# Mixture of experts over 64 experts: how the routing weights reach the tokens, and how far the down projection lags

## The reference, cut to what matters

```
xf = x.reshape(T, D)                                   # T = 4096, D = 128
shared = silu(xf @ Ws_up) @ Ws_down                    # F = 64
aff = xf @ centroids.T                                 # E = 64
_, idx = top_k(aff + expert_biases, 8)
w = sigmoid(take_along_axis(aff, idx)); w = w / (w.sum(-1) + 1e-8)
cw = zeros((T, E)).at[arange(T)[:, None], idx].add(w)
h = silu(einsum('td,edf->etf', xf, W_up))
y = einsum('etf,efd->etd', h, W_down)
out = x + shared + einsum('etd,te->td', y, cw)
```

## Time and profile before

| | us |
|---|---|
| median of 3 runs | 1128.03 (1126.86 to 1128.64) |
| the profiled execution | 1126.31 |
| its span, first to last instruction | 1124.5 |
| last stage | from 662.6 to the end |

### The profile page before, as it was taken

How to read it: one execution, slowest core, us unless ns; L and a number is a source line. 1 busy time by engine, 2 the same in 40 slices (tenths; PEclk the granted TensorE clock), 3 DMA queues, 4 the chain that set the end, 5 groups by cost and what they waited for, 6 DMA issues and landing times.

```text
span 1124.5 us, 20697 instructions
## 1 busy us (share of the span) xinstructions
PE 981.0 (87%) x6164; PEld 779.5 (69%) x6164; DVE 846.1 (75%) x1938; ACT 723.8 (64%) x1416; POOL 439.8 (39%) x503
## 2 busy tenths in 40 slices
PE   5665089999658999999999989999999999999998
PEld 3444079999536777776776667777777677777776
DVE  4865577777568888888887667878787768787865
ACT  4543045555347778778777667777777667777775
POOL 0266750000156556555553303333333333333343
PEclk9555589999869999999999989999999999999999
DMA  9011122222211101101010013241414140505050
GB/s 251 18 45 46 65 58 65 64 66 66 68 28 24 34 20 29 29 23 36 20 30 11 1 43 86 50 87 44 92 36 101 35 103 12 124 12 125 12 124 10
DMA packets 59749, 61.68 MB, mean 55 GB/s; under 512 B 15973, under 2 KB 54022, under 8 KB 57606
## 3 DMA queue, kind: packets, MB, share of 16 engines
q1 hardware_dynamic: 54976, 52.02, 19.4%
q0 software_dynamic: 4096, 8.40, 2.4%
q10 hardware_dynamic: 582, 0.09, 0.0%
HBM read 45.73 MB, written 14.75 MB: 54 GB/s over the span
## 4 chain that ended last, share of the span: by engine, by line
PE 74%; DVE 12%; ACT 5%; issue 5%; POOL 1%; DMA 1%; SPq 1%; DVEq 0%; POOLq 0%; ACTq 0%
PE ps L2070 5%; PE ps L2048 5%; PE ps L2050 4%; PE ps L2049 4%; PE ps L2072 4%; PE ps L2071 4%; PE ps L1848 4%; PE ps L1791 3%; PE ps L1911 3%; PE ps L2057 3%; PE ps L1866 3%; PE ps L1894 3%; PE ps L1872 2%; PE ps L1770 2%; PE ps L1769 2%
## 5 line engine op out<-in xcount | busy, mean ns | idle before, releaser
L741 POOL TENSOR_TENSOR hl<-h,hh 128x512 fp32r<-128x512 f32 x128 | 165.7, 1294 | 309.0 <-ACT hh L1017 309.0
L1017 ACT ACTIVATE hh<-h 128x512 fp32r<-128x512 f32 (+1 forms) x264 | 165.0, 625 | 17.4 <-DVE h L1634 16.1
L1534 DVE TENSOR_REDUCE nm<-ps 128x4 f32<-128x512 f32 (+1 forms) x128 | 116.3, 951 | 35.6 <-PE ps L1894 33.7
L1634 DVE TENSOR_TENSOR h<-sg,ps 128x512 f32<-128x512 f32 x160 | 108.2, 676 | 39.5 <-ACT sg L1005 37.9
L1005 ACT ACTIVATE sg<-ps 128x512 f32<-128x512 f32 x160 | 95.7, 598 | 54.4 <-PE ps L2050 54.2
L645 POOL DMA_INDIRECT yg<-ys,gps x64 | 63.0, 984 | 168.6 <-issue 158.1
L2070 PE MATMUL ps<-hh,wh 128*128 128x512 f32 x256 | 103.6, 405 | 18.0 <-DVE hl L1641 17.0
L2048 PE MATMUL ps<-xh,wh 128*128 128x512 f32 x256 | 105.8, 413 | 0.0
L1634 DVE TENSOR_TENSOR h<-ps,cwB 128x512 f32<-128x512 f32 x96 | 65.8, 685 | 50.2 <-ACT ps L1005 45.7
L1641 DVE TENSOR_TENSOR hl<-h,hh 128x512 fp32r<-128x512 f32 (+1 forms) x136 | 93.0, 684 | 13.6 <-ACT hh L1017 13.6
L2050 PE MATMUL ps<-xh,wl 128*128 128x512 f32 x256 | 102.7, 401 | 0.0
(11 more groups left out here) (320 smaller groups left out, 2741.1 us busy)
## 6 DMA issues: line engine op xcount, KB each, us to landing
cwB<-cwd SPq DMA_DIRECT2D x16, 1536.0 KB, 10.8
xb<-xs SPq DMA_DIRECT2D x72, 64.0 KB, 1.8
ys<-yb SPq DMA_DIRECT2D x72, 64.0 KB, 1.6
cwd<-cwS SPq DMA_DIRECT2D x32, 96.0 KB
x_res<-in_L_attn_x_dram SPq DMA_DIRECT2D x4, 512.0 KB, 9.1
wst<-in_L_ffn_W_up_dram SPq DMA_DIRECT2D x32, 64.0 KB, 2.2
wst<-in_L_ffn_W_down_dram SPq DMA_DIRECT2D x32, 64.0 KB, 1.9
out_dram<-y SPq DMA_DIRECT2D x8, 256.0 KB, 4.9
```

The source lines that it names most:

```text
L741: pool.tensor_tensor(hl4[:, u % 3, :], h4[:, u % 3, :], hh4[:, u % 3, :].bitcast(F32), op=ALU.subtract).then_inc(u_hlp, 1)
L1017: act.activation(hh4[r, u % 3, :], h4[r, u % 3, :], ACT.Copy).then_inc(u_hh, 1)
L1534: ins = dve.tensor_reduce(nm[:, u, 4 * g:4 * g + 4], o, axis=AX.X, op=ALU.max, negate=True)
L1634: dve.tensor_tensor(h4[:, u % 3, :], first, second, op=ALU.mult).then_inc(u_h, 1)
```

## The change

The diff has these parts in the last stage:

- NS goes from 20 to 8, NB from 12 to 24: units 1 to 8 are spread units, 9 to 32 are broadcast units.
- cwd has CWR = 4 copies instead of 8 and holds four pieces of 6 pairs (NPC); cwB has three buffers of 6 units (NBUF). SP writes with four DMAs of 48 rows each, then issues three loads (`spread_rows`) and the fourth (`rows_again`) once h of unit 14 has been made, since it goes to the buffer of the first. `e_h` waits for a load at units 9, 15, 21 and 27.
- Broadcast units rotate over five banks (0 to 4) for their up projections; spread units keep three and two.
- h and its two parts have five buffers (one of them for unit 0), and LAG is 4.
- The copy of the weights on DVE orders them by piece. cwS has 64 rows.

Beside it, the load of wuT (attention's output weights) moves behind the second stage and to other SBUF, and GpSimd's three semaphores for its own links become one.

```diff
-        NS = 20
+        NS = 8
         NB = NP2 - NS
         EP, EB = 2 * NS, 2 * NB
-        HB = 32
-        CWR = 8
-        assert EB <= HB and HB + 2 * EP <= P and NB % 2 == 0
-        cwd = nc.dram_tensor("cwd", [2, 2, 2, CWR, NB // 2 * TT], F32).ap()
+        HB = 64
+        CWR = 4
+        NPC, NBUF = 4, 3
+        G = NB // NPC
+        assert EB <= HB and HB + 2 * EP <= P and NB % NPC == 0
+        cwd = nc.dram_tensor("cwd", [2, NPC, 2, CWR, G * TT], F32).ap()
...
-        h4 = sb("h4", [P, 3, TT], F32)
-        hh4 = sb("hh4", [P, 3, TT], F32R)
-        hl4 = sb("hl4", [P, 3, TT], F32R)
+        h4 = sb("h4", [P, 5, TT], F32)
+        hh4 = sb("hh4", [P, 5, TT], F32R)
+        hl4 = sb("hl4", [P, 5, TT], F32R)
...
-        cwB = sb("cwB", [P, NB, TT], F32)
+        cwB = sb("cwB", [P, NBUF, G, TT], F32)
...
         def broadcast_unit(u):
 
-            return u > 8 and u % 2 == 1
...
+            return u > NS
+
+        def rows_of_unit(u):
+
+            piece, j = divmod(u - NS - 1, G)
+            return piece, piece % NBUF, j
...
+        def up_bank(u):
+
+            return u % 3 if u <= NS else (u - NS - 1) % 5
+
+        def spread_bank(u):
+
+            return 3 + u % 2
...
+        def slot(u):
+
+            return u % 4 if u else 4
...
-            sp_.dma_start(wuT[:, :], WuT).then_inc(c_in, 16)
...
+            sp_.dma_start(wuT[:, :], WuT).then_inc(sh_in, 16)
             sp_.dma_start(shf[:, 0:F2], Ws_up).then_inc(sh_in, 16)
...
+            def load_rows(t, piece):
+
+                sp_.dma_start(cwB[:, piece % NBUF, :, :].rearrange("p u t -> p (u t)"),
+                              cwd[t % 2, piece].rearrange("h r x -> (h r) x").unsqueeze(1).broadcast_to(
+                                  [2 * CWR, F2 // CWR, G * TT])).then_inc(rows_in[piece % NBUF], 16)
 
             def spread_rows(t):
 
                 sp_.wait_ge(d_cw, t + 1)
-                for g in range(2):
-                    for half in range(2):
-                        sp_.dma_start(cwd[t % 2, g, half].rearrange("r (e t) -> e r t", t=TT),
-                                      cwS[half * NB + g * G:half * NB + (g + 1) * G, :].unsqueeze(1).broadcast_to(
-                                          [G, CWR, TT])).then_inc(rows_out, 16)
-                sp_.wait_ge(rows_out, 64 * (t + 1))
...
+                for r in range(CWR):
+                    sp_.dma_start(cwd[t % 2, :, :, r, :].rearrange("k h x -> (k h) x"), cwS[0:EB, :]).then_inc(rows_out, 16)
+                sp_.wait_ge(rows_out, 16 * CWR * (t + 1))
+                for piece in range(NBUF):
+                    if t == 0 and piece == 0:
+                        sp_.wait_ge(c_PV, 4 * B)
+                        sp_.wait_ge(d_const, 2)
+                    if t == 0 and piece == 1:
+                        sp_.wait_ge(c_F1, 2 * B)
+                    if t == 0 and piece == 2:
+                        sp_.wait_ge(c_F5, B)
                     if t > 0:
...
+                        last = max(k for k in range(NPC) if k % NBUF == piece)
+                        sp_.wait_ge(u_h, (t - 1) * NP2 + NS + (last + 1) * G)
+                    load_rows(t, piece)
+
+            def rows_again(t):
+
+                for piece in range(NBUF, NPC):
+                    sp_.wait_ge(u_h, t * NP2 + NS + (piece - NBUF + 1) * G)
+                    load_rows(t, piece)
 
             spread_rows(0)
             for t in range(T // TT):
                 if t > 0:
                     sp_.wait_ge(u_y, t)
                     sp_.dma_start(out_tok[:, (t - 1) * SUB:t * SUB, :], y4[:, (t - 1) % 2, :, :]).then_inc(o_out[(t - 1) % 2], 16)
+                rows_again(t)
                 if t + 1 < T // TT:
                     spread_rows(t + 1)
...
+                    by_piece = cs[:, :, 0:EB].rearrange("p s (k h j) -> p s k h j", k=NPC, h=2)
+                    pairs = g4[:, 5, :, EP:E2].rearrange("p s (k j h) -> p s k h j", k=NPC, h=2)
                     for half in range(2):
-                        dve.tensor_copy(cs[:, :, half * NB:(half + 1) * NB], g4[:, 5, :, EP + half:E2:2])
+                        dve.tensor_copy(by_piece[:, :, :, half, :], pairs[:, :, :, half, :])
...
-            LAG = 3
+            LAG = 4
```

More of the change, by code:

```diff
@@ L257, in bass_two_layers @@
         ooT = sb2("ooT", [P, 2, P], F32)
+        wuT = sb2("wuT", [P, D], F32)
         attn.close()
@@ L386, in broadcast_unit, with rows_loaded, wait_bank, slot_before @@
         def broadcast_unit(u):
-            return u > 8 and u % 2 == 1
[L390 to L398, removed]
+            return u > NS
+        def rows_of_unit(u):
+            piece, j = divmod(u - NS - 1, G)
+            return piece, piece % NBUF, j
+        def rows_loaded(piece, t):
+            twice = piece % NBUF + NBUF < NPC
+            return 16 * (2 * t + 1 + piece // NBUF if twice else t + 1)
+        def up_bank(u):
+            return u % 3 if u <= NS else (u - NS - 1) % 5
+        def spread_bank(u):
+            return 3 + u % 2
+        BANKS_USED = [(use, u, bank_(u)) for u in range(NP2 + 1) for use, bank_, there in (
+            ("up", up_bank, True), ("spread", spread_bank, 0 < u <= NS)) if there]
+        def wait_bank(eng, t, use, u):
+            n = BANKS_USED.index((use, u, up_bank(u) if use == "up" else spread_bank(u)))
+            earlier = [(a, v, t) for a, v, k in BANKS_USED[:n] if k == BANKS_USED[n][2]]
+            if not earlier:
+                if isinstance(t, int) and t == 0:
+                    return
+                earlier = [(a, v, t - 1) for a, v, k in BANKS_USED if k == BANKS_USED[n][2]]
+            a, v, t_of = earlier[-1]
+            if v == 0:
+                eng.wait_ge(u_sg0, t_of + 1)
+            elif a == "spread" or broadcast_unit(v):
+                eng.wait_ge(u_h, t_of * NP2 + v)
+            else:
+                eng.wait_ge(u_sg, t_of * NP2 + v)
         def x4_bank(n):
             return bank[3] if isinstance(n, int) and n == 0 else bank[6]
+        def slot(u):
+            return u % 4 if u else 4
+        def slot_before(t, u):
+            if u >= 5:
+                return t, u - 4
+            return t - 1, (NU - 5 + u if u else 0)
         def is_split(eng, t, u):
-            if u < 0:
-                t, u = t - 1, NU + u
             if u % 2:
@@ L886, in x4_weights @@
                 if not (isinstance(n, int) and n == 0):
-                    act.wait_ge(rows_out, 64 * n)
+                    act.wait_ge(rows_out, 16 * CWR * n)
                 act.activation(cwT[:, p, :], x4_bank(n)[:, :], ACT.Copy)
@@ L1012, in e_hi @@
                     act.wait_ge(u_h, t * NP2 + u)
[L1013 to L1017, removed]
+                if u >= 5 or not (isinstance(t, int) and t == 0):
+                    last_t, last_u = slot_before(t, u)
+                    act.wait_ge(u_dn, last_t * NU + last_u + 1)
+                act.activation(hh4[r, slot(u), :], h4[r, slot(u), :], ACT.Copy).then_inc(u_hh, 1)
             def out_copy4(t, p):
@@ L1624, in e_h @@
                 if broadcast_unit(u):
[L1625 to L1628, removed]
-                else:
[L1630 to L1633, removed]
-                dve.tensor_tensor(h4[:, u % 3, :], first, second, op=ALU.mult).then_inc(u_h, 1)
+                    piece, buf, j = rows_of_unit(u)
+                    first, second = bank[up_bank(u)], cwB[:, buf, j, :]
+                    if j == 0:
+                        dve.wait_ge(rows_in[buf], rows_loaded(piece, t))
+                else:
+                    dve.wait_ge(u_cw, t * NS + u)
+                    first, second = sg4[:, u % 3, :], bank[spread_bank(u)]
+                if u >= 5 or not (isinstance(t, int) and t == 0):
+                    is_split(dve, *slot_before(t, u))
+                dve.tensor_tensor(h4[:, slot(u), :], first, second, op=ALU.mult).then_inc(u_h, 1)
             def e_lo(t, u):
@@ L2051, in e_up @@
                 if u > 0 and not broadcast_unit(u):
[L2052 to L2057 removed]
+                    wait_bank(pe, t, "spread", u)
+                    pe.matmul(bank[spread_bank(u)][:, :], selr[:, 2 * u - 2:2 * u, :].rearrange("p e f -> p (e f)"), cwT[:, p, :],
                               start=True, stop=True).then_inc(u_cw, 1)
```

88 lines of the change are left out of this document (33 added, 55 removed).

## The result

The changed kernel takes 1237.76 us (median of 4 runs, 1236.16 to 1239.12), the kernel before 1127.44 in the same comparison (1124.31 to 1128.64). The ratio is 1.0983, 95% interval 1.0955 to 1.1011: **9.8% slower**, where 1242.5 us had been forecast. The profiled execution took 1238.82 us, its span 1237.1.

A forecast was written before the change was run, and what follows sets the result against it. Bound before: TensorE in a tile's first half, the ScalarE-VectorE chain in its second. With slow loads, 727.6 us for the first tile's last load, 497 for seven tiles of 71.0, then the end: span 1239.4, median 1242.5, range 1180 to 1275.

The forecast's parts named there:

- A load's time: Last stage: each load of cwB runs on 8 engines, loads landing 13.6 us apart, bounds 12.0 to 14.2.
- Writes to loads: Tile's end: next first load follows the weights' writes after 7.1 us; 7.9 if unchanged, 5.6 with quicker issue.
- The tile: Last stage: one tile takes 12.4 + 16.8 + 3 x 13.6 + 1 = 71.0 us, where it was 56.3.
- Start and end: First tile's fourth load lands at 727.6 us, the last tile's at 1224.6; then 7.7, 5.1 and 2 us to the end.
- The waits: VectorE's h waits for loads of cwB at units 9, 15, 21 and 27 of each tile.
- TensorE and its clock: Last stage: TensorE busy below 80%; lower clock after gaps hidden between loads, costing 2 us at the end.
- Rival 4: Gaps hold TensorE at 1.2 GHz, six units need 15 us, more than a load's 13.6: 1275 us; chance 10%.
- Rival 1, all hidden: Every load lands before its unit, leaving TensorE's gain of 14 us: 1114 us; chance 9%.
- The predicted wait at unit 30: Tile's second half: with loads in time, TensorE still waits at unit 30 for the router's weights from VectorE's chain.
- The rival's condition: Loads spread over 16 engines after all, or eight engines carrying a load in under 9 us.
- The lag: Later down projection only lets TensorE run ahead; 0.7 us in the last tile, one down projection fewer before its last up projection.
- the five banks: Up projections of broadcast units: the two additional silu buffers in PSUM cost nothing; five banks gain nothing by themselves.

The follow-up runs named there:

- e8_ports: Changed kernel with each load as four transfers of 32 neighbouring partitions, still eight engines: 1123.23 us in one run, kernel before 1141.74 on that chip.
- e12_sixteen_by_two: As e8_ports, but each of the four transfers has 16 x 2 partitions, on sixteen engines: 1110.6 us in one run, kernel before 1126.79.
- e2_halves16: Changed kernel, CWR = 4 and the writes kept, each load in two transfers of 64 partitions: 1124.46 us, ratio 0.9837 to the kernel before.
- e5_cwr2: Changed kernel with CWR = 2 instead of 4, each load read from 4 rows of cwd: 1376.1 us in one run.
- e1_cwr8: Changed kernel with CWR = 8 instead of 4, each load read from 16 rows of cwd: 1124.42 us, ratio 0.9836 to the kernel before.
- e11_before_again: The kernel before, unchanged, profiled again beside the last comparison: 1127.17 us.
- e10_banks3_lag3: e2_halves16 with three banks for all up projections and LAG = 3: 1118.03 us, ratio 0.9929 to the kernel before.
- e7_lag3: e2_halves16 with LAG = 3 instead of 4: 1131.52 us, ratio 0.9921 to the kernel before.
- e9_banks3: e2_halves16 with three banks for all up projections, LAG still 4: 1109.21 us, ratio 0.9847 to the kernel before.
- e6_weights31: e2_halves16 with the router's weights turned at unit 31 instead of 30, their wait moved to unit 1: 1115.08 us, ratio 0.9762 to the kernel before.
- e3_before_cwr4: The kernel before with CWR = 4 instead of 8 and nothing else changed: 1157.78 us, ratio 1.0142 to the kernel before.

## Why the prediction was right

The time was 4.7 us off and the mechanism was the predicted one, but the steps were not all as good as their sum.

- **A load's time.** Predicted 13.6 us on 8 engines (12.0 to 14.2), measured 14.2 to 14.9 in most tiles, at and above the upper bound, and about 12.7 in the tile of 65.5. The eight small packets, the share of 0.49 and 110 GB/s were forecast. The reason that I gave was wrong: "a busy engine moves the same whether six or sixteen run", with the engine's own rate as the limit. e8_ports has engines at 25 GB/s, e12_sixteen_by_two has them at 13 again. What the rows fit is the number of SBUF ports written at a time, with two engines to each port in the slow shapes. The Trainium skill's page "SBUF — State Buffer", section "Door 1: The DMA port swizzle", puts four neighbouring partitions and the four 32 further on into one port, with 27.2 GB/s for each port. An estimate by this map takes for granted that each engine writes its own run of neighbouring partitions and that the engines stay in step; no row shows either. Then 8 ports are written at a time in the kernel before, in e2_halves16, e8_ports and e12_sixteen_by_two, and 4 in the changed kernel. The measured 217, 228, 206, 217 and 110 GB/s are 27, 29, 26, 27 and 27 GB/s a port. For e5_cwr2 it gives 2 ports; its first 61 GB/s are 31 a port, more than the page has, and its 105 GB/s would need engines that have left step. That was not tested by itself. The changed kernel shows the same in its tile of 65.5 us: from 905 to 935 us it moves 131 GB/s, a store with it, at the same share of 0.49. So the ports are the explanation that fits, foretold for e8_ports and e12_sixteen_by_two, but not shown beyond doubt. I had that section before me and wrote that no row shows ports. In the changed kernel CWR = 4 halves both the engines and the ports, so the wrong reason gave the right number; that was luck.
- **Writes to loads.** Predicted 7.1 us, measured 4.8 in most tiles: the writes' issue is 2.7 us and their data is the same 0.39 MB. The lower bound (5.6) was too high too.
- **The tile.** 5.3 + 7.1 + 16.8 + 41.8 = 71.0 was predicted, 5.6 + 4.8 + 17.4 + 43.9 = 71.7 measured for one; two misses of some 2 us cancel. The mean is 70.6.
- **Start and end.** The last load of the first tile: 727.6 predicted, 728.1 measured. That of the last tile: 1224.6 and 1221.73. From there to the end: 14.8 us, measured 1237.1 - 1221.7 = 15.4.
- **The waits.** Of h's waits of the changed kernel, 21 have a load as their releaser, and 10 of the same length no named one:

```profile
  DMA cwB<-cwd: 90.3, 21
  issue: 43.7, 10
```

  With 32 loads in the kernel this is nearly every load, as forecast.
- **TensorE and its clock.** TensorE is busy for 464.9 / 573.8 = 81% of the stage, and I had said below 80%. The clock of 0.90 does not show in the tiles, whose length the loads set; at the end the 15.4 us leave 2.6 for it, where 2 was put. Rival 4 didn't come. Its working was off too: six units at 1.2 GHz are 2 x 8.4 = 16.8 us, not 15, so its 1275 us was too low.
- **Rival 1, all hidden.** Its price was 14 us, e1_cwr8 gained 461.9 - 444.7 = 17.2 in the stage (15.6 against the 460.3 of e11_before_again). I took a tile of the kernel before as 56.3 us, has it, but six of them take 344.9, 57.5 in the mean, three of them with a clock of 0.94 to 0.97. That the price came near is luck: it was for the spreading alone, which is worth 8 us (e10_banks3_lag3 against the kernel before beside it), and the rest is the lag's, below. The tile with loads in time was 54.8 predicted and 55.0 measured. The predicted wait at unit 30 is there: the longest of the eight, 2.5 us, lies ahead of the first tile, the other seven are 1.4 us in the mean. The rival's condition, a load in under 9 us on eight engines, holds for e8_ports (7.3 to 8.5 us a load). The 23 GB/s that an engine had reached in the earlier trace rows pointed there. I set that row aside because "no transfer of this stage shows such a rate"; it was the row that the engine's limit could not explain.
- **The lag.** "The later down projection and the two more h buffers only let TensorE run ahead", worth nothing before the last tile. This failed. By e2_halves16 against e7_lag3 and e9_banks3 against e10_banks3_lag3 the lag is worth 7 to 10 us, about half of what the change gains when its loads are in time. The step that failed is that VectorE's chain alone sets the second half: TensorE's stall of 2.3 us and the clock that it sometimes costs were not in the sum. That the five banks bring nothing held.

With the loads in time the parts are: 0.7% for the spreading by transfers (e10_banks3_lag3, 0.9929), 0.8% for the lag (e9_banks3, 0.9847), nothing for the banks, and 0.75% more for turning the weights later (e6_weights31, 0.9762).

## What to carry over

Before a transfer is reshaped, work out from its outermost dimension how many engines it gets, and then which partitions those engines write at the same moment: here one constant halved both, and the runs speak for the second as what cost the rate. A rate per busy engine that differs between two rows of the same trace is a question, and a limit that explains only one of them is not yet found. Price a small stall with the clock it can cost, and compare tiles by their mean.

## What the runs showed of the hardware

- 32 neighbouring partitions took 206 GB/s from eight engines and 217 from sixteen; 25 to 26 GB/s was the most that an engine reached in these loads.
- A load from four engines moved 61 GB/s in its first 10 us; later in the same kernel four engines moved 105.
- After a stall of 2.3 us at the same place TensorE's granted clock was 0.63 over about four microseconds in one tile of e7_lag3 and 1.00 in the next.
- Halving the copies from eight to four shortened the issue of four writes from 4.4 to 1.9 us (e3_before_cwr4).
